# A two-layer graph network on one core: transposed rows written over x, 16 tiles not stored, four groups of moments

## The chip, the cores and the metric

One core of a Trainium2 chip runs the whole kernel. The metric is the device time of one launch in microseconds (us). Before the change it is 4124.46 us, the median of 3 runs (4123.27 to 4125.03).

## The reference, cut to what matters

x has 6250 nodes with 512 features; 100,000 edges (src, dst) are sorted by dst. A graph attention layer with 8 heads of 64 features and then two graph convolutions follow:

```python
h = maximum(layernorm(x), 0)
el = ((h @ W_src + b_src) * attn_l) summed over the 64 features of each head      # [N, 8]
er = ((h @ W_dst + b_dst) * attn_r) summed likewise                               # [N, 8]
v  = h @ W_val + b_val
e  = leaky_relu(el[src] + er[dst]); a = softmax of e over the edges with one dst
x  = x + segment_sum(v[src] * a, dst)
h  = maximum(layernorm(x), 0)
x  = x + relu(gcn(relu(gcn(h, W1, b1)), W2, b2))     # gcn gathers rows by src, too
```

The kernel folds attn into the weights (16 columns instead of 2 x 512), so that el and er come from one narrow product of h, and adds b_val at the end.

## The kernel before, in words

The nodes are cut into 49 tiles of 128 (`TILES`). On-chip memory is nearly full, so areas are reused: `big` (49 x 520 columns a partition) holds first x, then tables of the edge work, then the sums; `rows_wmat` holds 8 slots of 512 columns and the weights; `edge` holds the folding, the search, and later the scores of all edges. Every engine runs its own program in order and waits on semaphores.

**First pass (VectorE, ScalarE, TensorE, SyncE).** x arrives in chunks of 8 tiles, three issued by ScalarE, the rest by SyncE (L1005). VectorE takes the statistics of each tile (L466) and computes mean and deviation for a group of tiles at once (`moments`, L468; groups 0 to 7, 8 to 23, 24 to 48); ScalarE takes the root of a group in `deviations` (L1321). Tile after tile, ScalarE normalizes into one of two slots (L1333), TensorE transposes (`turn`, L1524), and ScalarE copies the transposed tile to one of four slots, `ht_out` (L1341). The copy waits until the score product (L1548) and the store to `ht_tab` of the tile four places before are done. The score product of tile t stands right behind the transpose of tile t + 1. Every four tiles ScalarE copies the 16 score columns (L1348) and TensorE turns them (L1556). The score product needs the folded weights: GpSimd multiplies weights with attn (L1206, L1207) once all six loads have landed, and VectorE reduces (L492, L494).

**Search (VectorE, GpSimd).** Where each node's edges begin is found in seven groups of seven tiles: VectorE counts among 255 row ends (`find_rows`, L510), GpSimd gathers one row of 391 dst for each node (L1216), VectorE counts in it (`count_in_rows`, L523), and every group but the first two waits for the counts of the second before it. The last count is followed by index work on VectorE, TensorE (L1579 to L1607) and SyncE.

**Values (TensorE, ScalarE).** v is computed tile by tile: ScalarE reloads the transposed tile from `ht_tab` into a ring of four slots in `big` (L1317), TensorE multiplies by W_val (`value`, L1566), ScalarE copies and stores to `v_tab` (L1361, L1365). The places are written out by hand: `V1` = 14 values before the picking loop, with the index steps between them (7, then 1, 1, 1, 1, 3), and 35 after it. Of these, 5 and then 6 up to `V_AT[0]`, 8 up to `V_AT[1]`, 10 up to `V_AT[2]`; each such place is followed by a carry step that VectorE's scans need. `EXP_AT` is the value before which ScalarE computes the exponentials (L1385), `W_AT` the value counts before each of the eight turns of the edge weights (L1650).

**Picking loop.** 145 steps for 580 of the 782 edge columns: TensorE gets el[src] by products with one-hot columns (L1621), VectorE picks the block (L684 to L697). Meanwhile GpSimd gathers the other 202 columns (`GCOLS`) from `el_tab` (L1239), paced by the loop.

**Edge stage, then gathers.** VectorE scans over all edges for er, the maxima, the exponentials' sums (L767 to L823). After the store of the sums it zeroes `big` in two parts (L838, L841). GpSimd starts gathering rows of v (L1280) when all values are stored; three stages of 782 gathers follow, each with a dense step between.

Of the kernel before, what the change touches and what calls it, by code (L numbers as in the profile page):

```python
# [68 lines left out]
GROUPED = (0, 8, 24, TILES)  # L69
# [5 lines left out]
Q = 4  # L75
# [47 lines left out]
def build(nc, x, src, dst, W_src, b_src, W_dst, b_dst, W_val, b_val, attn_l, attn_r, W1, b1, W2, b2, out):  # L123
    ctx = ExitStack()
    with ctx:
# [140 lines left out]
        below = part(SEEK * (ROW // 2 + 1)).bitcast(BF16).rearrange("p (s n) -> p s n", s=SEEK)  # L266
# [23 lines left out]
        scanned = part.at  # L290
        ht_ring = part(HT * D).rearrange("p (s n) -> p s n", s=HT)
        ringed = part.at
# [11 lines left out]
        g_from = part(CUT.blocks ** 2 * P // 2).bitcast(BF16).rearrange("p (g n) -> p g n", n=CUT.blocks * P)  # L304

# [6 lines left out]
        def ht_out(slot):  # L312
            return rows[:, (4, 5, 0, 1)[slot], :]
# [4 lines left out]
        def first(t):  # L318
# [15 lines left out]
        pad_set, const_set, ident_set, edges_kept, fold_in, edges_in, dst_in = map(sem, (  # L334
            "pad_set", "const_set", "ident_set", "edges_kept", "fold_in", "edges_in", "dst_in"))
# [11 lines left out]
        wval_in, fold_loads = fold_in, 6  # L347
# [13 lines left out]
        ht_kept, low_before = low_in, [16 * len(range(n, TILES, HT)) for n in range(HT)]  # L361
# [41 lines left out]

        def all_kept(eng, pair, per=16):
            eng.wait_ge(pair[0], per * ((TILES + 1) // 2))
            eng.wait_ge(pair[1], per * (TILES // 2))
# [17 lines left out]

        prep, pe_steps = [0], [0]
# [3 lines left out]
        def _(dve):  # L429
# [38 lines left out]
            def moments(n, at):  # L468
# [9 lines left out]
                dve.scalar_tensor_tensor(ln[:, 1, at], ln[:, 3, at], 0.25, ln[:, 2, at], ALU.mult, ALU.add).then_inc(ln_set, 1)  # L478
                dve.wait_ge(std_set, n + 1)
# [6 lines left out]
            moments(0, slice(0, GROUPED[1]))  # L486
            statistics(range(1, 2))

            for s in range(2):
# [6 lines left out]
            dve.wait_ge(folded, 10)  # L496
            statistics(range(2, 3))
            dve.wait_ge(stat_set, GROUPED[2])
            moments(1, slice(GROUPED[1], GROUPED[2]))

# [51 lines left out]
            moments(2, slice(GROUPED[2], TILES))  # L552
# [17 lines left out]

            dve.wait_ge(h_set, TILES)
# [233 lines left out]
            dve.wait_ge(std_set, 4)  # L805
# [204 lines left out]
        def _(sp):  # L1010
# [4 lines left out]
            sp.dma_start(W_src_sb[:, :, :], W_src.rearrange("(k p) n -> p k n", p=P)).then_inc(fold_in, 16)  # L1015
            sp.dma_start(attn_sb[:, 0, :], on_all(attn_l.rearrange("h f -> (h f)"))).then_inc(fold_in, 16)
            sp.dma_start(bsd_sb[:, 0, :], on_all(b_src)).then_inc(fold_in, 16)
            sp.dma_start(W_dst_sb, W_dst.rearrange("(k p) n -> p k n", p=P)).then_inc(fold_in, 16)
            sp.dma_start(attn_sb[:, 1, :], on_all(attn_r.rearrange("h f -> (h f)"))).then_inc(fold_in, 16)
            sp.dma_start(bsd_sb[:, 1, :], on_all(b_dst)).then_inc(fold_in, 16)  # L1020
# [22 lines left out]
            for t in range(TILES):  # L1043
                sp.wait_ge(hT_set, t + 1)
                sp.dma_start(ht_tab[t, :, :], ht_out(t % HT)).then_inc(ht_kept[t % HT], 16)
                if t in (8, 11):
                    sp.wait_ge(edges_kept, 64)
                    load_firsts((8, 11).index(t))
                if t == 22:
                    sp.dma_start(src_flat[:, 0:J], src_rows.rearrange("g e -> (g e)").rearrange(  # L1050
                        "(p j) -> p j", j=J)).then_inc(edges_in, 16)
                if t == 26:
                    sp.dma_start(dst_i, dst_flat).then_inc(dst_in, 16)
                if t == 30:
                    sp.wait_ge(folded, 10)
                    sp.dma_start(wmat[:, :, 0:D], W_val.rearrange("(k p) n -> p k n", p=P)).then_inc(wval_in, 16)
                if t == 36:
# [8 lines left out]
            sp.wait_ge(h_set, TILES)  # L1066
            sp.wait_ge(dve_prep, marks["ends_of_units"])
# [6 lines left out]
            for n in range(HT):  # L1074
                sp.wait_ge(ht_kept[n], 16 * len(range(n, TILES, HT)))
# [105 lines left out]
        def _(pool):  # L1181
# [37 lines left out]
            pool.wait_ge(h_set, TILES)  # L1219
# [90 lines left out]
        def _(act):  # L1310
# [5 lines left out]
            def load_ht(t, slot):  # L1316
                act.dma_start(ht_ring[:, slot, :], ht_tab[ds(t, 1), :, :].rearrange("a p n -> p (a n)")).then_inc(ht_in[slot], 16)  # L1317

            def deviations(n, at):
                act.wait_ge(ln_set, 9 * n + 7)  # L1320
                act.activation(ln[:, 3, at], ln[:, 1, at], ACT.Sqrt, bias=epsc[:, 0:1]).then_inc(std_set, 1)  # L1321
                act.wait_ge(ln_set, 9 * n + 9)
            deviations(0, slice(GROUPED[0], GROUPED[1]))
# [418 lines left out]
```

## Time and profile before

| | |
|---|---|
| median of 3 runs | 4124.46 us (4123.27 to 4125.03) |
| profiled execution | 4119.5 us, span 4117.6 us, granted clock 0.96 |
| busy, share of the span | TensorE 84%, GpSimd 64%, VectorE 55%, ScalarE 43% |
| chain that ended last | TensorE 33%, GpSimd 24%, issue 21%, DMA 12%, VectorE 6% |
| first pass and index work | 0 to 203.8 us |
| picking loop | 203.8 to 538.5 us |
| edge stage | 538.5 to 713.9 us |
| gathers and dense steps | 713.9 to 4117.6 us |

The profile is of one execution and 5 us below the median. Busy shares are means over stages with different limits; for a change in one stage the waits of that stage count. Only 5% of the span (0 to 203.8) is the first pass and its index work, where most of the edit lies.

### The profile page before, as it was taken

The page shows a single profiled execution, that of the slowest core. Times are in us where ns is not written, and L with a number is a line of the kernel's source. Part 1 is how long each engine was busy: PE and PEld are TensorE (multiplying, and loading weights), DVE is VectorE, ACT ScalarE, POOL GpSimd, SP SyncE. Part 2 cuts the span into 40 slices and gives each one's busy share as a digit, 9 for nine tenths or more (in the row PEclk, how much of TensorE's full clock was granted, in tenths as well). Part 3 has the DMA queues.
Part 4 walks back from the last instruction along what each step waited for, and adds up shares of the span by engine and source line. Part 5 has one row for each costly group of instructions (what it writes and reads, how often), then busy time and mean ns, then how long its engine had stood idle before and what let it go on. Part 6 is the DMA issues. An engine that isn't in the chain of part 4 may idle for free.

```text
span 4117.6 us, 54129 instructions
## 1 busy us (share of the span) xinstructions
PE 3452.2 (84%) x14584; PEld 1660.4 (40%) x14584; DVE 2261.8 (55%) x3808; ACT 1782.4 (43%) x4148; POOL 2652.6 (64%) x2781
## 2 busy tenths in 40 slices
PE   5899986777888888897788888888996788888887
PEld 4499943222233333343333333333442333333333
DVE  6599886677778888884222233333552222333336
ACT  4355512445445555454333344444343333444442
POOL 3676501777777777655777777777006777777775
PEclk9999998999999999999999999999998999999998
DMA  8833335777777777665777777777117777777779
GB/s 287 248 67 62 91 96 190 210 210 211 210 210 211 210 211 211 190 205 189 211 210 210 210 210 210 211 210 210 65 67 221 210 211 210 210 211 210 210 209 353
DMA packets 318135, 802.85 MB, mean 195 GB/s; under 512 B 74201, under 2 KB 97899, under 8 KB 316889
## 3 DMA queue, kind: packets, MB, share of 16 engines
q0 software_dynamic: 201216, 630.92, 53.4%
q1 hardware_dynamic: 87149, 115.33, 8.6%
q10 hardware_dynamic: 29580, 54.49, 3.8%
q8 instruction: 67, 1.10, 0.1%
q14 instruction: 123, 1.01, 0.1%
HBM read 713.14 MB, written 88.19 MB: 195 GB/s over the span
## 4 chain that ended last, share of the span: by engine, by line
PE 33%; POOL 24%; issue 21%; DMA 12%; DVE 6%; SPq 1%; POOLq 1%; DVEq 1%; ACT 1%; ACTq 0%
POOL edge L1280 19%; PE mm L1529 8%; DMA edge<-h_tab,src_group 6%; DMA rows_wmat<-v_tab,src_group 5%; POOL rows_wmat L1280 4%; PE sm L1693 4%; PE mm L1621 4%; PE tr L1621 4%; PE mm L1693 4%; PE sm L1566 3%; DVE edge L866 2%; PE tr L1693 2%; PE tr L1524 1%; DVE big L876 1%; DMA ht_tab<-rows_wmat 1%
## 5 line engine op out<-in xcount | busy, mean ns | idle before, releaser
L1280 POOL DMA_INDIRECT edge<-h_tab,src_group x1564 | 1483.7, 949 | 708.8 <-issue 447.2
L1436 ACT ACTIVATE hots<-iota,drel 128x128 f32<-128x128 f32 x1760 | 538.0, 388 | 1174.6 <-PE tr L1693 593.1
L1280 POOL DMA_INDIRECT rows_wmat<-v_tab,src_group x782 | 739.4, 945 | 289.3 <-issue 218.4
L1693 PE MATMUL mm<-edge,hots 128*128 x880 | 446.1, 654 | 195.5 <-SPq L1098 194.7
L1693 PE MATMUL sm<-edge,hots 128*128 x880 | 454.3, 664 | 155.8 <-SPq L1098 153.1
L891 DVE TENSOR_TENSOR big<-big,mm 128x512 f32 x220 | 151.2, 687 | 674.5 <-PE tr L1693 656.7
L891 DVE TENSOR_TENSOR big<-big,sm 128x512 f32 x220 | 151.2, 687 | 620.8 <-PE misc L1693 606.8
L1693 PE MATMUL tr<-edge,hots 128*128 x880 | 395.6, 592 | 0.0
L1693 PEld LDWEIGHTS mm<-edge,hots 128*128 128x128 f32 x880 | 175.7, 208 | 459.8 <-issue 459.8
L1529 PE MATMUL mm<-rows_wmat 128*128 128x512 f32 x784 | 356.8, 599 | 0.0
L1693 PEld LDWEIGHTS sm<-edge,hots 128*128 128x128 f32 x880 | 180.0, 211 | 422.9 <-issue 422.7
L1673 PE MATMUL mm<-edge,hots 128*128 128x512 f32 x592 | 276.2, 605 | 67.6 <-ACT hots L1422 42.4
L1673 PE MATMUL sm<-edge,hots 128*128 128x512 f32 x584 | 275.4, 602 | 54.4 <-issue 27.9
L866 DVE TENSOR_TENSOR edge<-rows_wmat,tr 128x1024 f32<-128x1024 f32 x224 | 271.9, 1215 | 83.6 <-SPq L1098 83.6
L1422 ACT ACTIVATE hots<-eler_hots,ones 128x256 f32<-128x256 f32 x440 | 223.6, 508 | 206.9 <-PE sm L1673 74.4
L866 DVE TENSOR_TENSOR edge<-rows_wmat,misc 128x1024 f32<-128x1024 f32 x216 | 262.5, 1215 | 80.5 <-SPq L1098 80.1
L1417 ACT ACTIVATE eler_hots<-iota,drel 128x128 f32<-128x128 f32 x880 | 298.2, 386 | 0.0
L1239 POOL DMA_INDIRECT edge<-el_tab,src_flat x202 | 193.3, 957 | 106.2 <-DVE rows_wmat L690 50.9
L1439 ACT ACTIVATE hots<-hots,ones 128x1024 f32<-128x1024 f32 x220 | 252.6, 1148 | 7.1
L1693 PEld LDWEIGHTS tr<-edge,hots 128*128 128x128 f32 x880 | 167.3, 190 | 211.9 <-issue 211.9
L1693 PE MATMUL misc<-edge,hots 128*128 x440 | 206.8, 592 | 0.0
L1693 PE MATMUL hist_ps<-edge,hots 128*128 x440 | 206.8, 592 | 0.0
(252 smaller groups left out, 4465.9 us busy)
## 6 DMA issues: line engine op xcount, KB each, us to landing
h_tab<-rows_wmat SPq DMA_DIRECT2D x98, 256.0 KB, 2.0
edge<-h_tab,src_group POOLq DMA_INDIRECT x1564, 3.7
rows_wmat<-low_tab SPq DMA_DIRECT2D x145, 128.0 KB
ht_tab<-rows_wmat SPq DMA_DIRECT2D x49, 256.0 KB
big<-ht_tab ACTq DMA_DIRECT2D x49, 256.0 KB, 2.8
v_tab<-rows_wmat ACTq DMA_DIRECT2D x49, 256.0 KB, 3.0
x_tab<-big SPq DMA_DIRECT2D x49, 256.0 KB, 2.1
rows_wmat<-v_tab,src_group POOLq DMA_INDIRECT x782, 3.7
```

The source lines that it names most:

```text
L866: dve.tensor_tensor(msgs[:, k % MSGS, :, :].rearrange("p c (h f) -> p c h f", f=F), got, weights.unsqueeze(3).to_broadcast([P, 2, H, F]), ...
L891: dve.tensor_tensor(big[:, ds(o, D)], big[:, ds(o, D)], agg_ps[bank][:, :], ALU.add).then_inc(a["acc_added"], 1)
L1239: pool.indirect_dma_start(el[:, at, :], None, el_tab, bass.IndirectOffsetOnAxis(ap=src_flat[:, at:at + 1], axis=0)).then_inc(el_in[n // AH ...
L1280: pool.indirect_dma_start(ring[:, 2 * u + c, :], None, tab, bass.IndirectOffsetOnAxis(ap=src_group[:, n:n + 1], axis=0)).then_inc(a["rows_ ...
L1417: act.activation(dist[:, n % 2, c, :], iota[:, :], ACT.Abs, bias=drel[:, n * 2 + c:n * 2 + c + 1], scale=-1.0).then_inc(a["dist_set"], 1)
L1422: act.activation(onehot[:, n % HOTS, :, :], dist[:, n % 2, :, :], ACT.Relu, bias=ones[:, 0:1], scale=-1.0).then_inc(a["onehot_set"], 1)
L1436: act.activation(group_hots[:, q % 2, e, :], iota[:, :], ACT.Abs, bias=drel[:, col:col + 1], scale=-1.0).then_inc(a["dist_set"], 1)
L1439: act.activation(group_hots[:, q % 2, :, :], group_hots[:, q % 2, :, :], ACT.Relu, bias=ones[:, 0:1], scale=-1.0).then_inc(a["onehot_set"], 1)
L1529: last = nc.tensor.matmul(bank, rows[:, slot, k * P:(k + 1) * P], rhs(k), start=(k == 0), stop=(k == KC - 1))
L1621: last = pe.matmul(sum_ps[bank][:, q * NA * H:(q + 1) * NA * H], src_hot[:, par, kt, q * P:(q + 1) * P], el_parts[:, part, kt, :, :], star ...
L1673: last = pe.matmul(gat_ps[w % GAT_SUMS][:, :], onehot[:, w % HOTS, n, :], msgs[:, w % MSGS, n, :], start=(n == 0), stop=(n == 1))
L1693: last = pe.matmul(agg_ps[bank][:, :], group_hots[:, q % 2, w % GROUP * 2 + n, :], edge[:, ds(slot[w % OFFS] + n * D, D)], start=(n == 0), ...
```

## The change: what it does

- `ht_out` and its ring of four are gone. ScalarE copies the transposed tile over x, `first(t)` in `big`, without waiting for a store or a product. SyncE stores only tiles 0 to 32 (`STORED`). The score product of tile t now stands behind the transpose of tile t + 12 (`LAGGED`), and the small turns seven steps later.
- Values go in the order of `V_ORDER`: first tiles 33 to 48, read from `big` where they lie, then 0 to 32, reloaded. `V1` becomes 16. The ring of reloads moves from `big` to four slots of `rows_wmat`; two of these are in use in the picking loop, so their first reload is issued at its end.
- Groups of moments: 0 to 7, 8 to 15, 16 to 31, 32 to 48. `moments` is cut in two, `moments` and `scales`, and ScalarE takes the root one step earlier. Folding is done side by side: each side needs three loads. VectorE's order is written anew, with the parts of the search between the statistics. GpSimd waits for the fold before it gathers.
- The places `V_AT`, `EXP_AT`, `W_AT` and SyncE's small loads are shifted. `all_ht_kept` (a wait for all stores) guards `big` before it is reused. Zeroing covers 2048 columns less on VectorE and more on GpSimd.

```diff
-GROUPED = (0, 8, 24, TILES)
+GROUPED = (0, 8, 16, 32, TILES)
-V1 = 14
-V_AT = (V1 + 11, V1 + 19, V1 + 29)
-EXP_AT = (V1 + 25, V1 + 25)
-W_AT = (V1 + 32, V1 + 32, V1 + 33, V1 + 33, V1 + 34, V1 + 34, TILES, TILES)
+STORED = 33
+V1 = TILES - STORED
+LAGGED = 12
+V_AT = (V1 + 11, V1 + 18, V1 + 28)
+EXP_AT = (V1 + 23, V1 + 23)
+W_AT = (V1 + 31, V1 + 31, V1 + 32, V1 + 32, TILES, TILES, TILES, TILES)
+V_ORDER = (*range(STORED, TILES), *range(STORED))
...
-        ht_ring = part(HT * D).rearrange("p (s n) -> p s n", s=HT)
-        ringed = part.at
+        scanned = ringed = part.at
...
-            return rows[:, (4, 5, 0, 1)[slot], :]
+        def reloaded(slot):
+            return rows[:, (6, 7, 2, 3)[slot], :]
...
+            dve.wait_ge(stat_set, GROUPED[2])
+            moments(1, at_group[1])
+            fold_side(0)
+            scales(1, at_group[1])
             turned()
-            for g in range(4):
-                find_rows(g)
-            statistics(range(GROUPED[2] // XL, TILES // XL))
+            find_rows(0)
+            fold_side(1)
+            statistics(range(2, 4))
+            dve.wait_ge(stat_set, GROUPED[3])
+            moments(2, at_group[2])
+            find_rows(1)
+            scales(2, at_group[2])
+            statistics(range(GROUPED[3] // XL, TILES // XL))
...
-            moments(2, slice(GROUPED[2], TILES))
+            moments(3, at_group[3])
+            find_rows(2)
+            scales(3, at_group[3])
+            find_rows(3)
+            dve.wait_ge(folded, 10)
...
-            for t in range(TILES):
+            for t in range(STORED):
                 sp.wait_ge(hT_set, t + 1)
-                sp.dma_start(ht_tab[t, :, :], ht_out(t % HT)).then_inc(ht_kept[t % HT], 16)
+                sp.dma_start(ht_tab[t, :, :], first(t)).then_inc(ht_kept[t % HT], 16)
...
+                if t == 14:
+                    sp.wait_ge(folded, 10)
+                    sp.dma_start(wmat[:, :, 0:D], W_val.rearrange("(k p) n -> p k n", p=P)).then_inc(wval_in, 16)
...
-            pool.wait_ge(fold_in, 16 * fold_loads)
             for s, w in enumerate((W_src_sb, W_dst_sb)):
+                pool.wait_ge(fold_in[s], 16 * fold_loads)
...
             pool.wait_ge(edges_kept, 64)
+            pool.wait_ge(folded, 10)
...
-                    if t >= HT:
-                        act.wait_ge(eler_sum, t - (HT - 1))
-                        act.wait_ge(ht_kept[t % HT], t // HT * 16)
-                    act.activation(ht_out(t % HT), tr[t % 2][:, :], ACT.Copy).then_inc(hT_set, 1)
+                    act.activation(first(t), tr[t % 2][:, :], ACT.Copy).then_inc(hT_set, 1)
...
+            values(0, V1 - 1)
+            all_ht_kept(act)
+            act.wait_ge(eler_turned, -(-TILES // 4))
+            for n in range(2):
+                load_ht(n)
+            values(V1 - 1, V1)
...
-                if 1 <= k <= TILES:
-                    t = k - 1
+                if LAGGED <= k < TILES + LAGGED:
+                    t = k - LAGGED
...
+            def value(c):
+                t = V_ORDER[c]
+                if c < V1:
+                    pe.wait_ge(hT_set, t + 1)
+                    source = first(t)
+                else:
+                    pe.wait_ge(ht_in[t % HT], t // HT * 16 + 32)
+                    source = reloaded(t % HT)
```

## Rows read from the trace of the kernel before

**Rows 1.** Busy us (instructions) by engine in stages; then clock, DMA share, GB/s.
```profile
56.40:138.50 82.10, 75.70 (x564) 53.41 (x562) 63.62 (x223) 58.51 (x96) 46.40 (x49) 0.93 0.79 271
...
203.80:538.50 334.70, 326.87 (x6960) 325.78 (x6960) 298.69 (x862) 192.25 (x288) 204.72 (x216) 0.98 0.31 69
...
713.90:1700.00 986.10, 805.77 (x1759) 298.89 (x1760) 781.66 (x878) 494.31 (x1356) 743.12 (x786) 0.99 0.73 209
```

**Rows 2.** The chain of waits: start us, us, what (whole kernel).
```profile
145.88 25.92 PE sm L1566 x56
...
587.87 30.20 PE sm L1566 x64
619.65 20.81 PE sm L1566 x48
...
688.19 8.87 DVE big L838
699.80 4.67 PE sm L1566 x8
```

**Rows 3.** Who waited for whom, 56.4 to 138.5 (us in total, times, longest).
```profile
ACT rows_wmat L1341 <- DMA ht_tab<-rows_wmat: 11.6, 6, 4.6
```

**Rows 4.** Timeline to 57: start, us, engine, line, out<-in [idle before <-releaser].
```profile
23.99 4.85 DVE L466 BATCH_NORM_STATS2 big<-big  x8 [6.03 <-DMA big<-x]
26.82 1.27 POOL L1206 TENSOR_TENSOR edge<-edge 128x512 f32<-128x512 f32 x1 [23.08 <-DMA edge<-L_gnn_b_dst]
...
31.89 2.46 DVE L492 TENSOR_REDUCE rows_wmat<-edge 128x8 f32<-128x512 f32 x4 [3.05 <-POOL edge L1207]
...
40.69 1.89 PE L1548 MATMUL sm<-rows_wmat 128*16 128x128 f32 x8 [19.85 <-DVE blr L494]
...
53.99 1.12 PE L1524 MATMUL tr<-ident,rows_wmat 128*128 128x128 f32 x4
...
55.04 1.89 PE L1548 MATMUL sm<-rows_wmat 128*16 128x128 f32 x8
...
56.47 0.81 ACT L1333 ACTIVATE rows_wmat<-big,small 128x512 f32<-128x512 f32 x1 [0.53 <-DVE small L482]
```

**Rows 5.** Timeline, 58 to 173: the pass at full clock, the search, index work.
```profile
58.49 0.66 PE L1524 MATMUL tr<-ident,rows_wmat 128*128 128x128 f32 x4
...
59.08 1.05 PE L1548 MATMUL sm<-rows_wmat 128*16 128x128 f32 x8
...
59.30 0.17 DVE L513 CAST er_idx<-small 128x7 int32<-128x7 f32 x1
...
60.06 0.42 PE L1556 MATMUL mm<-ident,rows_wmat 16*128 16x16 f32 x4
...
61.82 0.95 POOL L1216 DMA_INDIRECT edge<-dst_rows,er_idx  x1 [0.30 <-issue]
...
138.50 1.04 DVE L566 TENSOR_TENSOR eler_hots<-mm,blr 128x512 f32<-128x512 f32 x2 [11.36 <-PE mm L1556]
...
172.41 0.21 DVE L613 COPY small<-misc 128x49 f32<-128x49 f32 x1 [11.84 <-PE misc L1580]
```

**Rows 6.** Timeline of the edge stage, 618 to 720.
```profile
618.40 0.41 DVE L713 COPY big<-misc 8x256 f32<-8x256 f32 x1 [3.83 <-PE misc L1657]
...
632.50 6.87 DVE L803 TENSOR_TENSOR edge<-edge 128x3128 f32<-128x3128 f32 x2
...
641.49 1.28 ACT L1385 ACT_TABLE_LOAD   x1 [0.41 <-ACT rows_wmat L1361]
...
660.60 0.38 PE L1657 MATMUL misc<-ident,tail_st 128*8 128x128 f32 x2 [4.58 <-DVE tail_st L812]
...
706.73 3.60 PE L1566 MATMUL sm<-rows_wmat,big 128*128 128x512 f32 x8
...
713.88 0.95 POOL L1280 DMA_INDIRECT rows_wmat<-v_tab,src_group  x1 [51.36 <-DMA v_tab<-rows_wmat]
714.29 5.18 DVE L841 MEMSET big<- 128x6144 f32 x1 [1.91 <-issue]
```

More of the change, by code:

```diff
@@ L402, in all_landed, with all_ht_kept @@
                     eng.wait_ge(pair[b], 16 * n)
+        def all_ht_kept(eng):
+            for n in range(HT):
+                eng.wait_ge(ht_kept[n], low_before[n])
         def all_kept(eng, pair, per=16):
@@ L485, in _, with fold_side @@
             dve.wait_ge(stat_set, GROUPED[1])
-            moments(0, slice(0, GROUPED[1]))
+            moments(0, at_group[0])
+            scales(0, at_group[0])
             statistics(range(1, 2))
-            for s in range(2):
+            def fold_side(s):
                 dve.wait_ge(dve_setup, 2 * s + 2)
@@ L1380, in _ @@
             pipelined(act, PCOLS // Q, 4, 0, far)
+            act.wait_ge(el_picked, PCOLS // Q)
+            for n in range(2, HT):
+                load_ht(n)
             def exponentials(half):
@@ L1530, in product @@
                 last.then_inc(done, 1)
-            for k in range(TILES + 8):
+            for k in range(TILES + LAGGED + 7):
                 if k < TILES:
@@ L1548, in _ @@
                         last = pe.matmul(sm[q % 2][0:2 * H, n * P:(n + 1) * P], wmat[:, kc, D:D + 2 * H],
-                                         ht_out(t % HT)[:, kc * P:(kc + 1) * P], start=(kc == 0), stop=(kc == KC - 1))
+                                         first(t)[:, kc * P:(kc + 1) * P], start=(kc == 0), stop=(kc == KC - 1))
                     last.then_inc(eler_sum, 1)
-                if k >= 8 and k % 4 == 0:
-                    q = k // 4 - 2
-                    pe.wait_ge(elerT_set, q + 1)
-                    for t in range(4 * q, min(4 * q + 4, TILES)):
-                        at = t % (D // (2 * H)) * 2 * H
-                        last = pe.transpose(mm[t // (D // (2 * H))][:, at:at + 2 * H], elerT[:, q % 2, t % 4 * P:(t % 4 + 1) * P],
-                                            ident[0:2 * H, 0:2 * H])
-                    last.then_inc(eler_turned, 1)
@@ L1560, in value @@
-            def value(s):
-                t, par = s.k, s.j % 2
-                pe.wait_ge(ht_in[s.j], (t - s.j) * 4 + 32)
-                if s.past(2):
-                    pe.wait_ge(v_set, t - 1)
+                if k >= LAGGED + 7 and (k - LAGGED - 7) % 4 == 0:
+                    q = (k - LAGGED - 7) // 4
+                    if q * 4 < TILES:
+                        pe.wait_ge(elerT_set, q + 1)
+                        for t in range(4 * q, min(4 * q + 4, TILES)):
+                            at = t % (D // (2 * H)) * 2 * H
+                            last = pe.transpose(mm[t // (D // (2 * H))][:, at:at + 2 * H], elerT[:, q % 2, t % 4 * P:(t % 4 + 1) * P],
+                                                ident[0:2 * H, 0:2 * H])
+                        last.then_inc(eler_turned, 1)
@@ L1565, in value @@
+            pe.wait_ge(elerT_set, -(-TILES // 4))
+            def value(c):
+                t = V_ORDER[c]
[5 more added lines that the diff above has]
+                    source = reloaded(t % HT)
+                if c >= 2:
+                    pe.wait_ge(v_set, c - 1)
                 for k in range(KC):
-                    last = pe.matmul(sm[par][:, :], ht_ring[:, s.j, k * P:(k + 1) * P], wmat[:, k, 0:D],
+                    last = pe.matmul(sm[c % 2][:, :], source[:, k * P:(k + 1) * P], wmat[:, k, 0:D],
@@ L1571, in values @@
             def values(n):
-                for t in range(values_done[0], values_done[0] + n):
-                    value(Step(t, t % HT, TILES, False))
+                for c in range(values_done[0], values_done[0] + n):
+                    value(c)
                 values_done[0] += n
-            pe.wait_ge(wval_in, 16 * (fold_loads + 1))
+            pe.wait_ge(wval_in, 16)
             values(7)
```

104 lines of the change are left out of this document (49 added, 55 removed).

## The prediction

> **What bounds the kernel now.** I read the busy table by stage first [rows 1]. From 713.9 to 1700 GpSimd issues row gathers at 1.25 us each (0.95 busy, 0.30 between), 743 us busy of 986. The two later gather stages are of the same kind, and nothing after 713.9 is edited. So the change can only move the start of that first gather, and what it moves is handed on one to one. The question is what the first 713.9 us wait for.
>
> The chain of waits [rows 2] answers in four pieces. (a) The first pass over the 49 tiles of x ends at 138.5. (b) TensorE then computes "values" (h times W_val, 8 matmuls a tile, 3.45 us at full clock: 20.81/6), 56 matmuls without a break from 145.88, and its index work stands behind them; the picking loop starts at 203.8 [rows 1]. (c) That loop, 203.8 to 538.5, is TensorE at 327 us of 335; it is not edited. (d) From 538.5 VectorE scans and TensorE's values alternate on the chain: the blocks of 64 and 48 matmuls at 587.87 and 619.65 are values, 688.19 is the zeroing of the sums, and 699.80 the value before the last.
>
> In the first pass the tiles pass ScalarE and TensorE; the list of waits shows that ScalarE stood 11.6 us in six waits for the store of an older transposed tile after 56.4 [rows 3]. The timeline shows the start [rows 4]: statistics of chunk 1 at 23.99, the folding product on GpSimd only at 26.82 (after six loads), the first score product at 40.69, tile 8's normalization at 56.47. At full clock a tile costs TensorE 0.59 us for the transpose and 0.98 for the score product (start of one to start of the next, 58.49 and 59.08), and every fourth tile 0.34 to 0.42 more [rows 5].
>
> **The change, part by part.**
>
> *Moments in four groups, fold in two halves.* VectorE now runs: statistics of chunk 1 to 28.8, moments 0.95, fold of one side 3.1 (four reductions 2.46, one 0.68), scales 0.5, one part of the search 3.1 (56.35 to 59.47), fold of the other side 3.1. GpSimd's first product took 5.1 us (26.82 until VectorE took it at 31.89 [rows 4]) and the second somewhat more; the second can still only start at 26.8, so both are ready by 33 and hide. The folds end at 39.8, against 40.6: no gain there. But tiles 8 to 15 get their scale at 33.4 instead of 56.4, and need no score product before them, since that now lags 12 tiles. ScalarE takes 1.43 us a tile (58.5 us busy for 41 tiles [rows 1]), so they are through by 45. Then it is idle again: two chunks of statistics (9.7), moments, a part of the search and the scales put tile 16 at 54.2. The pass is then 8 transposes further than before but has only 4 score products done.
>
> *Rest of the pass.* 33 transposes at 0.59, 45 score products at 0.98 and 13 small turns at 0.34: 19.5 + 44.1 + 4.4 = 68 us from 54.9. I add 2 us for a slow start (a tile at the lower clock costs 1.05 + 1.8 [rows 4], and the clock is low for one or two tiles after a pause) and 1 for the last handshake: end at 126, before 138.5. What makes 82 us become 71: 11.6 us of store waits are gone (the copy goes over x, no ring), and 8 transposes (4.7 us) are done early, against 4 more score products still owed (3.9). The stores that remain (33 of 256 KB) have nothing waiting on them before 126, and SyncE can issue the first 16 from 42 on; at the stage's 271 GB/s they need 32 us. The copy's new target and the product's new source are not in the trace: nearest rows 0.60 and 1.05, and I take no difference.
>
> *Search for rows.* It starts at 39.8 (GpSimd waits for the fold, whose area it overwrites) instead of 61.8, pauses from the second group (ends 62.5) for VectorE's count at 76, and 35 gathers of 1.25 after it are through by 125 at worst, when counts delay it. Not late.
>
> *Values without a reload.* The 7 values before the index product need no DMA: they start at 126.2, behind the pass, and end at 150.4 (7 x 3.45). Before, they started at 145.88 and the product was followed by VectorE at 172.41, which had stood 11.84 us [rows 5]: VectorE was done at 160.6, 22.1 us after the pass. Now that is 148.1, so TensorE is still last, by 2 us. Shift: 171.6 - 150.4 = 21.2 us. Then the order to the picking loop is the old one with two values more (16 instead of 14): +6.9. The loop starts 14.3 us earlier. Its own time stays; the gathered columns and their pacing are the same. The two reloads into slots that the loop occupies are issued at its end, 7 us before TensorE needs them.
>
> *Values between the scans.* The second block shrinks from 8 to 7. VectorE stood 3.83 us at 618.40 for TensorE [rows 6], so one value less gives min(3.45, 3.8) = 3.4 us. Then the exponentials are placed one value sooner after it (5 instead of 6). ScalarE began them at 641.49, 0.41 us behind its copy of a value, while their argument was there at 635.9 (half of the 6.87 from 632.50); a value less gives 3.4 us. TensorE had then 4.58 us to spare at 660.60, of which 1.1 is left: enough.
>
> *End.* Two values stood behind the zeroing of the sums, which ended at 697.1 [rows 2]; the gathers at 713.88 waited 51 us for GpSimd, released by the store of the second. Now only one stands there, so the last store leaves at the end of the product at 699.80 + 4.67 instead of 706.73 + 3.60: 5.9 us. VectorE's last zeroing (6144 columns, 5.18 us) shrinks to 4096 (3.45) and starts earlier too; the first product of gathered rows can't be due before two gathers and a landing, some 5 us behind the first gather, so it is covered, and would cost at most 2 us if not.
>
> Sum: 14.3 + 3.4 + 3.4 + 5.9 = 27.0 us. The profiled execution took 4119.5 us, which becomes 4092.5. The median of the runs is 4124.46, 5 above it, and I forecast against it: 4097.5.
>
> By the Trainium skill's "TensorE: Matmul & The Clock Gate" (section on the HAM clock gate) the low clock is the default and only activity lifts it, which speaks against the new pause of TensorE from 45 to 54. The trace agrees on the size, 3.0 us at low clock for transpose and score product against 1.71 [rows 4, 5]; by the rule alone the cost would be the second rival below.
>
> **Rivals.**
> 1. *Only the first half and the end pay.* If TensorE or ScalarE fills the 3.8 and 4.6 us of slack differently (values stall on their stores, or the exponentials hold ScalarE while TensorE needs its banks), the two 3.4 us are lost: 4104. If VectorE's index chain were not earlier at all, it would be ready at 160.6 and the loop would gain 171.6 - 160.6 - 6.9 = 4.1 instead of 14.3: 4108, or 4114 with both.
> 2. *The clock stays low in the pass (slower).* Place: TensorE from 54.2. A tile there costs 1.3 us more at the low clock, a score product of the tail 0.8. For all 33 tiles and the tail that is 52 us, 25 us net slower: 4150. It decides from 21 tiles on. Against it: after every pause before, two tiles were enough, and the pass had 0.93 of the clock granted [rows 1].
> 3. *Nothing arrives.* If something besides values held the loop or the gathers (the 9 us landing of tables, the sums' store), the gain would be taken up: 4120. The waits named in rows 5 and 6 speak against it.
> 4. *More.* Without slow start, and with the idle time before tile 16 shorter than I count: 4088.
>
> **How the numbers follow.** Forecast as summed, within 6 us: 0.60. Rival 1: 0.20. Rival 4: 0.08. Rival 3: 0.06. Rival 2: 0.04. The rest, 0.02, is a slowdown that I don't see. The cost of the slow start (0 to 6 us) and rival 1 set the range 4086 to 4114, which leaves out under 2 in 10. A measurement of this kernel tells about 0.2%, 8 us, from no change. Rival 3 and part of rival 1's far end lie within it: same 0.08; slower 0.05; faster 0.87.
>
> **What would show it.** In the profile after: the last score turned near 126; no wait of the copy for a store; tile 16's normalization near 54; the first value straight behind the pass; VectorE's wait for the index product near 2 us instead of 11.8; the picking loop at 189 to 190, as long as before; VectorE's wait after the second block near nothing; the exponentials right behind their argument; the first gather near 687, one value after the zeroing. I am wrong if the loop starts after 200, or if the gathers start earlier by 27 us and the rest takes it back.

## The result, and the profile after

The changed kernel takes 4104.6 us by the median of four executions (4099.5 to 4112.6), beside 4124.7 for the kernel before on the same chip: 20.1 us less, ratio 0.995 (0.9937 to 0.9962). A second set of five gave 4099.8 beside 4117.7, ratio 0.9949 (0.9935 to 0.9962). The forecast was 27.0 less, 4097.5: the first median lies 7.1 above it and inside the stated range (4086 to 4114), the second 2.3 above. The profiled execution took 4099.5 (span 4097.7) against 4119.5 (span 4117.6), 19.9 less by the spans.

**Stages.** The first view is the busy table, columns as in [rows 1]: the pass from tile 16 on, the picking loop, the first gather stage.

```profile
56.00:123.90 67.90, 67.49 (x544) 50.14 (x542) 52.31 (x184) 48.66 (x81) 32.07 (x35) 0.99 0.71 241
187.60:527.50 339.90, 327.54 (x6960) 326.02 (x6960) 297.55 (x863) 192.24 (x288) 206.74 (x217) 0.98 0.30 68
688.60:1676.00 987.40, 809.61 (x1768) 300.59 (x1767) 780.62 (x879) 495.95 (x1360) 745.26 (x786) 0.99 0.72 208
```

TensorE is busy 67.5 of 67.9 us in the pass (before: 75.7 of 82.1). The loop starts 16.2 us earlier than before (187.6 for 203.8), yet it and its exit (the stretch from the last full step to VectorE's first instruction behind the loop) need 340 us for the same 327 of TensorE, 5 more than the 335 of before. The first gather starts 25.3 us earlier (688.55 for 713.88), and of these 19.9 arrive at the end.

**The start.** Timeline of after to 60, columns as in [rows 4].

```profile
17.59 1.26 POOL L1226 TENSOR_TENSOR edge<-edge 128x512 f32<-128x512 f32 x1 [13.84 <-DMA edge<-L_gnn_b_src]
...
27.04 4.51 POOL L1227 TENSOR_TENSOR edge<-edge 128x2048 f32<-128x2048 f32 x1
27.98 3.60 DVE L478 TENSOR_TENSOR small<-big 128x8 f32<-128x8 f32 x1
35.61 0.81 ACT L1356 ACTIVATE rows_wmat<-big,small 128x512 f32<-128x512 f32 x1 [1.79 <-DVE small L493]
...
41.02 0.68 DVE L506 TENSOR_REDUCE blr<-edge 128x8 f32<-128x512 f32 x1
...
42.53 1.64 PE L1574 MATMUL sm<-big,rows_wmat 128*16 128x128 f32 x8
...
53.30 1.11 PE L1550 MATMUL tr<-ident,rows_wmat 128*128 128x128 f32 x4 [6.00 <-ACT rows_wmat L1356]
...
55.76 0.81 ACT L1356 ACTIVATE rows_wmat<-big,small 128x512 f32<-128x512 f32 x1 [2.04 <-DVE small L493]
```

Tile 8 is scaled at 35.61 (forecast 33.4), the folds end at 41.7 (39.8), tile 16 is scaled at 55.76 (54.2). The 2 us are one row: an addition of 8 columns on VectorE that takes 3.60 us and ends with GpSimd's product of 2048 columns (27.04 + 4.51). The same line took 0.17 us at 16.41, before GpSimd's first product. The 6.00 us in which TensorE stands are not the wait for tile 16, as I took them to be, but for tile 15, whose normalization stands on ScalarE behind the root of the next group.

**From the pass to the loop.** The same view (timeline) of the later stretch, columns as in [rows 5].

```profile
80.06 0.26 DVE L491 RECIPROCAL small<-small 128x17 f32<-128x17 f32 x1 [9.93 <-ACT small L1343]
...
123.94 1.04 DVE L586 TENSOR_TENSOR eler_hots<-mm,blr 128x512 f32<-128x512 f32 x2 [1.28 <-PE mm L1583]
...
133.31 1.77 POOL L1237 DMA_INDIRECT edge<-dst_rows,er_idx  x1 [0.30 <-issue]
...
147.97 0.32 PE L1612 MATMUL misc<-small,shift 128*128 128x49 f32 x2
...
152.70 0.63 PE L1620 MATMUL misc<-ident,edge 128*128 128x128 f32 x4 [0.44 <-DVE hist L637]
...
187.56 4.63 PE L1654 MATMUL mm<-big,edge 128*128 128x104 bf16 x67 [2.88 <-ACT edge L1401]
```

The pass ends at 123.94 instead of 138.50 [rows 5] and no copy waits for a store. The chain of waits of after (columns as in [rows 2]) runs elsewhere than before:

```profile
111.73 3.88 DVE hots L530 x14
133.31 3.73 DMA edge<-dst_rows,er_idx
139.67 3.88 DVE hots L530 x14
167.32 17.38 PE sm L1599 x40
```

Up to 78 it is still TensorE's pass; from 80.5 to 143.5 it is VectorE's counts and GpSimd's gathers for the search, the last of which ends at 135.1; at the end it is the five values in a row that stand last before the loop.

**The edge stage.** Timeline, columns as in [rows 6].

```profile
519.10 0.88 DVE L705 TENSOR_SCALAR edge<-rows_wmat,low_id 128x512 bf16<-128x512 f16 x3 [10.84 <-remote]
527.56 1.14 DVE L761 TENSOR_SCALAR big<-big,tile 128x256 f32<-128x256 int32 x4
...
603.42 0.41 DVE L734 COPY big<-misc 8x256 f32<-8x256 f32 x1 [0.54 <-PE misc L1690]
617.54 6.87 DVE L824 TENSOR_TENSOR edge<-edge 128x3128 f32<-128x3128 f32 x2
623.07 1.28 ACT L1411 ACT_TABLE_LOAD   x1 [0.39 <-ACT rows_wmat L1375]
642.23 0.38 PE L1690 MATMUL misc<-ident,tail_st 128*8 128x128 f32 x2
679.08 1.97 PE L1683 MATMUL tr<-ident,edge 128*128 128x128 f32 x8 [11.68 <-DVE edge L855]
680.85 4.21 PE L1599 MATMUL sm<-rows_wmat 128*128 128x512 f32 x8
688.55 0.95 POOL L1302 DMA_INDIRECT rows_wmat<-v_tab,src_group  x1 [44.40 <-DMA v_tab<-rows_wmat]
691.91 3.47 DVE L862 MEMSET big<- 128x4096 f32 x1 [1.75 <-issue]
696.92 2.35 DVE L887 TENSOR_TENSOR edge<-rows_wmat,tr 128x1024 f32<-128x1024 f32 x2 [1.53 <-SPq L1118]
```

And three rows of before at the loop's exit, from its timeline:

```profile
528.56 0.88 DVE L684 TENSOR_SCALAR edge<-rows_wmat,low_id 128x512 bf16<-128x512 f16 x3 [3.85 <-remote]
533.23 0.88 DVE L684 TENSOR_SCALAR edge<-rows_wmat,low_id 128x512 bf16<-128x512 f16 x3 [2.67 <-PE tr L1621]
539.25 0.88 DVE L740 TENSOR_SCALAR big<-big,tile 128x256 f32<-128x256 int32 x3
```

Up to its wait "remote" (a wait for which the profile names no releaser) VectorE needs 321.0 us of the loop in before and 320.7 in after; from there to the first instruction behind the loop (539.25, 527.56) it needs 14.5 and 19.3. So the steps cost the same and the exit is dearer. VectorE's one row does not measure this: before waits a second time, 2.67 us for TensorE, and after doesn't.

Behind the exit 11.7 us are left (16.2 less 4.5), the wait at the second carry falls from 3.83 to 0.54, the exponentials are 18.4 earlier [rows 6], and the first gather 25.3.

### The profile page after: what moved, and what is told of

Same layout as the page of the kernel before. It is cut to its first block, busy times and chain, and to the rows that moved or that the text cites. A ratio compares the mean times of both kernels' runs of the same rounds, so it can differ in the third digit from the quotient of the medians.

```text
span 4097.7 us, 54022 instructions
## 1 busy us (share of the span) xinstructions
PE 3458.8 (84%) x14584; PEld 1665.2 (41%) x14584; DVE 2264.1 (55%) x3817; ACT 1782.7 (44%) x4149; POOL 2664.8 (65%) x2781
## 4 chain that ended last, share of the span: by engine, by line
PE 31%; POOL 25%; issue 21%; DMA 13%; DVE 8%; POOLq 1%; ACT 1%; DVEq 1%; ACTq 0%; SPq 0%
POOL edge L1302 19%; PE mm L1555 8%; DMA rows_wmat<-v_tab,src_group 6%; POOL rows_wmat L1302 5%; DMA edge<-h_tab,src_group 5%; PE sm L1726 4%; PE mm L1654 4%; PE tr L1654 4%; PE mm L1726 3%; DVE edge L887 2%; PE tr L1726 1%; PE sm L1599 1%; PE tr L1550 1%; PE hist_ps L1726 1%; PE misc L1726 1%
## 5 line engine op out<-in xcount | busy, mean ns | idle before, releaser
L1726 PE MATMUL mm<-edge,hots 128*128 x880 | 457.9, 669 | 206.0 <-SPq L1118 204.8
```

Of the source, the lines that this page charges most:

```text
L1726: last = pe.matmul(agg_ps[bank][:, :], group_hots[:, q % 2, w % GROUP * 2 + n, :], edge[:, ds(slot[w % OFFS] + n * D, D)], start=(n == 0), ...
```

## The experiments

Lines are those of after. Where an expectation speaks of idle time "ahead of tile 16", it is the 6.00 us above.

**before_again and after_again**, both kernels unchanged.

> The kernel before, unchanged, looked at once more. What differs between the two profiles of before and after in code that the change did not touch: the first three thousand row gathers (median 946 ns before, 949 after), and the stall of all engines at the exit of the picking loop (VectorE stood 3.85 us there before, 10.84 after). Theory A, both belong to one execution: this profile shows another median gather than 946 ns by 2 ns or more, and another stall than 3.9 us by 2 us or more. Theory B, they belong to the kernel (its code and its addresses): 946 ns and 3.9 us come again, within 1 ns and 0.5 us.

> The kernel after, unchanged. Time 4104.5 by its median so far; single executions between 4099 and 4113. Theory A (run to run): the loop exit costs VectorE another time than 10.84 us, by 2 us or more, and the median gather is not 949 ns again. Theory B (the kernel's own): 10.8 us and 949 ns come again, and the first gather starts at 688.5 within 1 us.

4119.6 us (one execution) and 4099.8 (median of five). VectorE stood 4.19 and 10.74 us at the exit. The median gather is 946 ns in both, where the first profile of after had 949. The mean gather of the first and of the later stages is 945 and 949 ns in before_again, as in before, and 946 and 950 in after_again, where the first profile of after had 948 and 952. From the first gather to the last the profiles need:

```
before 3367.9   before_again 3369.0   over_x 3368.1   after 3375.4   after_again 3368.8
```

So the 7 us that the first profile of after lost in the gathers belong to that execution (theory A, in after alone). The stall at the exit belongs to the kernel (theory B): 4.19 for 3.85 and 10.74 for 10.84. Of the two repeats the first gather is at 714.25 and 689.69: 24.6 us earlier.

**over_x**, in the kernel before:

```
-  act.wait_ge(eler_sum, t - (HT - 1)); act.wait_ge(ht_kept[t % HT], t // HT * 16)
-  act.activation(ht_out(t % HT), tr[t % 2][:, :], ACT.Copy)
+  act.activation(first(t), tr[t % 2][:, :], ACT.Copy)      # stores and score products read first(t)
+  # VectorE, SyncE and GpSimd wait for all stores before they write big again
```

> The kernel before with one part of the change: the transposed row is written over its tile of x, scored and stored from there, so the copy waits for no older store and no older score product. All 49 tiles are still stored and read again, groups of moments, fold, lag of one and all places as before. Theory 1 (what the prediction counted): the 11.6 us of waits for stores are pure loss on TensorE's path; the pass then ends at 127 instead of 138.5. Theory 2: the stage is bound by TensorE's work after 56 us and by the DMA of x and of the rows together; the waits only moved the stores, which now queue behind the pass, and the reload (which waits for all of them) ends less than 4 us earlier. The first 56 values start at 145.88 before: by theory 1 at 134, by theory 2 at 142 or later. The whole by theory 1: 10 to 12 us less (ratio 0.9972), if VectorE's index chain, 11.8 us ahead at 172.41, allows it; by theory 2 under 4 us (0.999 to 1.000).

4113.0 us (4110.8 to 4118.6, n = 11) beside 4117.7: ratio 0.9985 (0.9976 to 0.9994). Timeline of over_x:

```profile
127.00 1.04 DVE L566 TENSOR_TENSOR eler_hots<-mm,blr 128x512 f32<-128x512 f32 x2 [5.22 <-PE mm L1557]
...
135.18 5.46 PE L1567 MATMUL sm<-rows_wmat,big 128*128 128x512 f32 x6 [8.21 <-DMA big<-ht_tab]
...
162.96 0.21 DVE L615 COPY small<-misc 128x49 f32<-128x49 f32 x1 [13.22 <-PE misc L1581]
```

Theory 1 holds for the stage and not for the whole: the pass ends at 127.0, 11.5 us earlier, and the values start at 135.2 behind 8.2 us of reload, but the median is only 4.7 less instead of 10 to 12 (ratio 0.9972 lies outside the interval). One of TensorE's waits in before, from its timeline:

```profile
113.38 1.89 PE L1548 MATMUL sm<-rows_wmat 128*16 128x128 f32 x8 [3.59 <-ACT rows_wmat L1341]
```

That the 11.5 meet the 11.6 of ScalarE's waits is partly luck. From its first score product to the pass's end TensorE itself stood three times in before (3.08, 2.77 and 3.59 us, 9.4 in all) and once in over_x (3.3). Behind such a wait tiles run at the low clock (the product above takes 1.89 us instead of 1.05): from 56.4 to the pass's end the granted clock was 0.93 in before and 0.98 in over_x, which I estimate at 5.7 and 1.4 us lost. So 6.1 of the 11.5 are waits and some 4 are clock.

Against before_again 9.9 us are left at the loop (194.31), 8.4 at the first gather (705.84) and 9.4 at the last; this kernel's loop exit is slower too (below).

**old_places**, in after:

```
-V_AT = (V1 + 11, V1 + 18, V1 + 28)
-EXP_AT = (V1 + 23, V1 + 23)
-W_AT = (V1 + 31, V1 + 31, V1 + 32, V1 + 32, TILES, TILES, TILES, TILES)
+V_AT = (V1 + 11, V1 + 19, V1 + 29)
+EXP_AT = (V1 + 25, V1 + 25)
+W_AT = (46, 46, 47, 47, 48, 48, TILES, TILES)
```

> The kernel after with the places of values, exponentials and weight turns as they were before: 8 values in the second block instead of 7, the exponentials 25 values in instead of 23, two values behind the zeroing of the sums instead of one. The prediction's terms: second carry +3.4 us (VectorE waits about 3.9 instead of 0.54 before it), exponentials +3.4 (they start 0.4 behind a copy instead of with their argument), first gather +5.9. Sum 12.7, first gather at 701 and time 4117. Rival: some of it overlaps (ScalarE waits with the exponentials for their argument anyway), and the sum is 6 to 9.

4108.5 us (4104.4 to 4111.8, n = 6), 8.7 over after. Its timeline:

```profile
606.36 0.41 DVE L734 COPY big<-misc 8x256 f32<-8x256 f32 x1 [3.16 <-PE misc L1690]
629.44 1.28 ACT L1411 ACT_TABLE_LOAD   x1 [0.39 <-ACT rows_wmat L1375]
```

With its loop exit at 527.87 (0.3 later than after), the second carry is worth 2.6 us, the exponentials 3.4 more (6.1 together), and the first gather, at 701.38, 6.4 more: 12.5 in all, as forecast (12.7). They add; the rival falls. The last gather is 11.7 later than in after_again. The medians show less (8.7), but they scatter by as much as the difference.

**lag5**, in after:

```
-LAGGED = 12
+LAGGED = 5
```

> The kernel after with the score products 5 tiles behind the transposes instead of 12. Theory 1 (the one I hold since the trace of after): from 56 us to the pass's end TensorE works without a gap (67.6 busy of 68.0), so the pass ends earlier by what TensorE gets done before. With a lag of 12 it stands idle for 6.0 us ahead of tile 16 while 8 score products are owed; with 5 it would fill that time: pass ends at 118 to 120 instead of 123.8. Theory 2 (the change's own ordering is right): the lag keeps tiles 8 to 15 free of the folds, and with 5 TensorE stands before the first score product from 29 to 42 and has ten transposes more to do behind it; the pass ends at 124 or later, up to 130. What the whole gains by theory 1 is bounded by VectorE, which has 0.4 us to spare before the turns of the low bits: 0 to 5 us; by theory 2 it loses 0 to 7.

4103.3 us (4100.0 to 4105.0, n = 5), 3.5 more than after_again (on another chip; the first gather, at 695.72, is 6.0 to 7.2 later than in the two profiles of after). Timeline of lag5:

```profile
85.64 0.27 DVE L491 RECIPROCAL small<-small 128x17 f32<-128x17 f32 x1 [11.58 <-ACT small L1343]
...
150.08 0.50 PE L1612 MATMUL misc<-small,shift 128*128 128x49 f32 x2 [3.65 <-DVE small L615]
...
151.09 6.68 PE L1599 MATMUL sm<-rows_wmat,big 128*128 128x512 f32 x8
```

Neither theory as written. TensorE had its last score turned at 122.1, 1.7 earlier, but ScalarE's last root came 5.6 us later (behind more tiles at TensorE's pace), VectorE's counts with it, and TensorE then waited for the positions: 3.65 us, and one value behind the wait took 6.68 instead of 3.70. The loop began at 193.9, 6.3 later than in after. So what bounds this stage in after is the search on VectorE and GpSimd, as the chain above says, and the lag of 12 pays by letting ScalarE reach that root early.

**last_value**, in after:

```
-W_AT = (V1 + 31, V1 + 31, V1 + 32, V1 + 32, TILES, TILES, TILES, TILES)
+W_AT = (V1 + 31, V1 + 31, V1 + 32, TILES, TILES, TILES, TILES, TILES)
```

> The kernel after with the last value ahead of the fourth weight turn instead of behind it. TensorE stands idle from 667.4 to 679.1 there, for VectorE's copies behind its 8.9 us zeroing; a value takes 4.2. Theory 1: the last value's store, and nothing else, starts the gathers: the first gather starts at 676 to 678 instead of 688.5 (-12), the gathers then run out of ring buffers after 12 of them (15 us, at 691) until VectorE's first message, which comes at 692 to 693 instead of 696.9, since TensorE's last turns follow at once. Net gain 6 to 10 us. Rival: the first gathers are held by VectorE and the weights anyway, the ring fills and what was gained is given back: under 3 us.

4091.1 us (five executions from 4088.1 to 4095.2; a sixth took 6261 at a mean granted clock of 0.73, and its cause is open), ratio 0.9931 (0.9918 to 0.9944), 8.7 less than after. GpSimd's rows:

```profile
673.07 0.95 POOL L1302 DMA_INDIRECT rows_wmat<-v_tab,src_group  x1 [28.85 <-DMA v_tab<-rows_wmat]
...
696.36 0.94 POOL L1302 DMA_INDIRECT rows_wmat<-v_tab,src_group  x1 [8.61 <-DVE edge L887]
```

The gathers start 15.5 us earlier, twelve of them fill the ring, and the thirteenth waits 8.6 us for the first message: the thirteenth is at 696.4, where in after it is at 703.6. The last gather is 10.3 earlier than in after_again. Theory 1, and the first gather 3 to 5 us earlier than it said: the product ended at 669.6, not 671.6, and the gather followed 3.5 us behind, as in after.

**two_after**, in after (all other places keep their numbers):

```
-V1 = TILES - STORED
+UNSTORED = TILES - STORED
+V1 = UNSTORED - 2
...
+  pool.wait_ge(v_sum, UNSTORED)            # ahead of GpSimd's zeroing of big
-  if c >= V1 and V_ORDER[c] + HT < STORED:
+  if c >= UNSTORED and V_ORDER[c] + HT < STORED:
-  if c < V1:
+  if c < UNSTORED:
```

> The kernel after with 14 instead of 16 values ahead of the picking loop; the last two unstored tiles stay in place and their values follow the loop. Theory: VectorE has its first picks ready at 168 to 170 and stands 21.3 us, so the loop is held by TensorE's five values in a row (167.25 to 184.7) alone: it starts 6.9 us earlier, at 180.7. Behind it TensorE has 4.64 us to spare before the first carry and now needs 6.9: 2.3 given back. First gather 4.6 us earlier than 688.5, whole 4 to 5 us less. Rival: VectorE or the far hot vectors of ScalarE (which wait for their table's landing) hold the loop at 185 or later, and the two values are then pure cost behind it: 0 to +2 us.

4093.7 us (4090.0 to 4094.9, n = 5). The loop starts at 180.50 (7.1 earlier, as forecast: nothing but TensorE's values held it), VectorE leaves it at 520.62; but the third carry stands at 642.82 (642.23 in after) and the first gather at 689.38. TensorE then had almost no gap between 521 and 643 (2.5, 1.6 and 2.4 us), so the 7 us were spent at the exponentials and the third carry, where VectorE now stood 3.5 us for TensorE (0.54 in after), and not the 2.3 at the first. The median is 6 us under after's all the same, which the first gather does not explain; the scatter of both is that large.

**padded**, in after, ahead of L1546:

```
+  for _ in range(32):
+      pe.matmul(hist_ps[:, 0:1], ones[0:1, :], lasts[:, 0:1], start=True, stop=True)
```

> The kernel after with 32 one-column matmuls on TensorE at its start, where it idles from 10.6 to 19.8 us: no work is changed, but TensorE's program is longer ahead of the picking loop. It asks what makes all engines stand at the loop's exit, 10.7 us in after and 9.3 in over_x but 3.9 to 4.2 in before. Theory A (where TensorE's instructions lie in memory when it leaves the loop): the stall changes by 2 us or more, and the whole with it. Theory B (something else of the stage): it stays 10.4 to 10.9 us, and the time is that of after.

4098.3 us (4094.8 to 4099.7, n = 5), ratio 0.9946 (0.9934 to 0.9959), that of after. VectorE stood 7.34 us at the exit instead of 10.74 to 10.84, but part of it came back in TensorE's next gaps. From the first match of the loop (TensorE's first product in it) to VectorE's first instruction behind it, in all profiles:

```
before 335.5, 335.0   best 337.5   over_x 337.7   padded 338.6   filled 339.7   old_places 339.9
after 340.0, 340.2    two_after 340.1   moved 340.3   last_value 340.4   lag5 340.5   burst 340.7
```

So instructions added on TensorE ahead of the loop, in time in which it is idle, change the exit by 1.5 us, more than the 0.5 us by which a repeat differs. best, which differs from moved in TensorE's and ScalarE's first pass only, is 2.8 under it. That this comes from where the instructions lie, and that it makes the whole 4.6 us between before and after, is a guess that no run settles. VectorE's own row is a bad measure of it, as two rows of two_after show:

```profile
505.87 0.88 DVE L706 TENSOR_SCALAR edge<-rows_wmat,low_id 128x512 bf16<-128x512 f16 x3 [4.58 <-remote]
...
513.18 0.88 DVE L706 TENSOR_SCALAR edge<-rows_wmat,low_id 128x512 bf16<-128x512 f16 x3 [5.32 <-PE tr L1656]
```

Its wait "remote" is 6 us shorter than in after, and a second wait takes it all back.

**moved**, in two_after:

```
-V_AT = (UNSTORED + 11, UNSTORED + 18, UNSTORED + 28)
-EXP_AT = (UNSTORED + 23, UNSTORED + 23)
-W_AT = (UNSTORED + 31, UNSTORED + 31, UNSTORED + 32, UNSTORED + 32, TILES, TILES, TILES, TILES)
+V_AT = (UNSTORED + 10, UNSTORED + 17, UNSTORED + 26)
+EXP_AT = (UNSTORED + 22, UNSTORED + 22)
+W_AT = (UNSTORED + 29, UNSTORED + 30, UNSTORED + 30, TILES, TILES, TILES, TILES, TILES)
```

> The kernel after with the values placed where TensorE has room: 14 ahead of the picking loop (as in two_after), 12, 7 and 9 ahead of the three carries instead of 11, 7 and 10, the exponentials 5 values behind the second carry as before, and in the turns of the weights one value between the first and the second, three between the third and the fourth (TensorE stands 3.7 and 11.7 us there in after). Theory: two_after lost its 7 us at the exponentials and the third carry, which stood behind too many values, so that TensorE had no gap from 521 to 643; last_value won 15.5 us at the first gather, of which GpSimd stood 8.6 for a free ring buffer, so its last value may be 3 to 6 us later for nothing. Both together: third carry at 636 instead of 642.2, first message 7 us earlier than last_value's 694.3, time 4083 to 4086. Rival: the two do not add, since TensorE becomes the bound between the loop and the third carry (two_after's 4.8 us stay lost): 4089 to 4092.

4084.2 us (4079.2 to 4087.6, n = 4) beside 4120.5, ratio 0.9911 (0.9895 to 0.9926). The parts add: loop at 181.82, third carry at 638.1 (forecast 636), and

```profile
672.66 0.95 POOL L1304 DMA_INDIRECT rows_wmat<-v_tab,src_group  x1 [32.64 <-DMA v_tab<-rows_wmat]
690.28 5.74 DVE L888 TENSOR_TENSOR edge<-rows_wmat,tr 128x1024 f32<-128x1024 f32 x5 [1.53 <-SPq L1119]
692.30 0.94 POOL L1304 DMA_INDIRECT rows_wmat<-v_tab,src_group  x1 [4.94 <-DVE edge L888]
```

the thirteenth gather is at 692.3, 11 us earlier than in after. The last gather is 12.6 earlier than in after_again. The first message came 4.1 earlier than last_value's 694.34, not 7.

**burst** is after with the tiles scored in step k of TensorE's first loop changed; **best** is burst and moved; **filled** is moved with its own steps and one value more ahead of the turns of the low bits (the small turns are moved to match in all three):

```
-after:   k - 12
+burst:   k = 12 to 15: k - 12;   k = 16, ahead of the turn: 4, 5, 6, 7;   from 17: k - 9
+filled:  k = 12 to 14: k - 12;   k = 15, ahead of the turn: 3, 4, 5, 6;   from 16: k - 9
+filled:  values(2)               # for values(1) ahead of the wait for marks["low"]
```

> The kernel after with four of the eight score products that are owed done in one go ahead of the transpose of tile 16, in the 6.0 us in which TensorE stands idle for its scales; behind it the lag is 9 instead of 12. Unlike lag5 this leaves tiles 8 to 15 ahead of the products and ScalarE's root of the last group where it was. Theory: the pass ends 4 us earlier (119.8 to 120.5 instead of 123.8), and the index product follows by what VectorE allows; lag5 ended the pass at 122.1 and lost 3.7 us there, because the last root came 5.6 us later. If the root comes at 80 again, the loop starts 2 to 4 us earlier (184 to 186) and the time is 4096 to 4098. Rival: VectorE was in step with TensorE at the index product and at the low bits (0.4 us to spare), so the loop starts at 187 again: 4100.

> burst and moved together. If their gains add: 6 to 12 us under after's 4099.8 for the one and 2 to 4 for the other, 4080 to 4084 in all; if VectorE holds the index product, as moved alone.

> moved, with the idle time of TensorE in the first pass really filled. In burst the four products stood behind the transpose of tile 15, which itself waits (tile 15's normalization stands on ScalarE behind the root of its group), so they ran at 54.7 instead of from 47.3 on, and the last root came at 83.8 instead of 80.1. Here the products of tiles 3 to 6 stand ahead of the transpose of tile 15, the lag is 9 from tile 16 on, and one value more stands ahead of the turns of the low bits, since VectorE, which waits for GpSimd's gathers of rows (their counts end at 143.5), has those bits at 152.4 whenever the pass ends. Theory: idle time before tile 15 falls from 6.0 to about 2, the pass ends at 120 instead of 124, the last root comes at 80 to 81, and the picking loop starts 3 to 4 us earlier than moved's 181.8: 178, time 4079 to 4082. Rival 1: VectorE's counts are the bound, the loop starts at 181 to 182: as moved, 4084. Rival 2: the low clock behind the filled stretch or a later last root takes it back: 184 and 4086.

burst took 4098.6 us (4097.4 to 4102.8, n = 5), best 4083.6 (4081.5 to 4087.2), filled 4085.4 (4083.7 to 4087.0, n = 4; ratio 0.9904, 0.9888 to 0.9921). In burst TensorE still stood 5.7 us for tile 15 and did the four products behind that tile's transpose, from 54.7 on; the pass ended at 124.2 and not at 120, the last root came at 83.75, VectorE was late for the low bits by 3.4, and the loop began at 190.8: the theory failed, by the wrong tile. best began its loop at 184.15, 2.3 later than moved, and got 2.8 back by its shorter exit. In filled the products ran from 47.7 on; 1.4 and 2.7 us of idle time stayed, the pass ended at 123.0 (moved: 124.9), the last root came at 82.3, and the loop began at 179.1, 2.7 earlier than in moved. VectorE's first message is 4.3 earlier and the last gather 2.1 (4043.8 for 4045.8). The medians of moved, best and filled can't be told apart. Filling TensorE in the pass bought next to nothing in these runs, as one expects where the other chain bounds the stage.

## Why the prediction was right, and where it was off

- *Fold in halves, groups of moments*: right that the folds gain nothing (41.7 for 39.8). Tile 8 came 2.2 us late, tile 16 1.6 late, by VectorE's 3.60 us row, which I had at 0.2. By the Trainium skill's "SBUF — State Buffer" (section "SBUF: two separate sides") VectorE and GpSimd share a port pair that one instruction holds until it ends; a VectorE instruction with two inputs in SBUF takes part beside a GpSimd instruction that reads SBUF. The two rows above agree: GpSimd's started first, and they end 0.03 us apart.
- *Rest of the pass*: forecast 126, measured 123.9. From the first transpose of tile 16 at 56.63 (forecast 54.9) it took 67.3 us, against the 68 of work alone: of the 3 us for the slow start and the handshake nothing was needed. 11.5 us of the gain are the ring's (over_x), 3.1 the groups, the lag and the rest together. The ring's term, 11.6, was read off ScalarE's waits and hit by luck: of the 11.5 only 6.1 are waits of TensorE, and most of the rest is its clock, which the term does not name.
- *Search for rows*: wrong by 10 us. The forecast "through by 125 at worst", which the sum relied on for VectorE's chain, became 135.1, because the counts for which the third group of gathers waits ended near 88 and not at 76. In before it ended at 139.0, only 3.9 later.
- *Values without reload*: right, the first follows the pass at once, and the index product is at 147.97 (150.4 forecast), 23.7 earlier. But one term failed: VectorE's index chain was to be done 22.1 us after the pass, at 148.1. It was done at 151.6, 27.7 after it and 9.0 earlier than before, since the search held it. VectorE came behind the product instead of 2 us ahead of it, and this cost only TensorE's wait of 0.44 us at the low bits, because a value stood in between: luck, as burst (a wait of 3.4) and lag5 (3.65) show. Loop 16.2 earlier for 14.3.
- *"Its own time stays"*: the step that failed and cost the most. The loop's steps took their time, its exit 4.5 us more (335.5 to 340.0). In every kernel with a changed first pass, over_x too, the exit is dearer than in before (337.5 to 340.7), though no line of the loop was edited. The cause is open.
- *Places*: 3.4 + 3.4 + 5.9 forecast, 2.6 + 3.4 + 6.4 by old_places. TensorE's slack at the third carry went from 4.58 to nothing, which cost nothing yet.
- *Gathers one to one*: right by repeat (24.6 at the first gather, 24.8 at the last). The recorded medians show 20.1 and 17.8: executions of after scatter from 4093 to 4113, and the first profile spent 7 us more in gathers that are not edited. What makes an execution of this kind is open.

So the sum is 16.2 - 4.5 + 3.3 + 3.4 + 6.9 = 25.3 for the forecast 27.0. The two errors inside it cancel in part: 1.9 us more at the loop than forecast, 4.5 less behind it. Rival 1 (second half fails) and 3 (nothing arrives) fall by old_places. Rival 2 falls too: from 56 to 124 the granted clock was 0.99. Of rival 4 half came true: no slow start, but the idle time before tile 16 was longer and not shorter. By the first gather the parts are: ring 8.4, places 12.5, and what is left of 24.6, 3.7, unstored tiles, groups and lag together.

## What to carry to other kernels

A wait counted on one engine is not what its removal gives on another: count the waits and the clock of the engine that bounds the stage. When one engine's stage has been shortened, read the chain of waits anew before shortening it again: here the pass went from TensorE to the search on VectorE and GpSimd, and three attempts to fill TensorE (lag5, burst, filled) gave nothing that the medians show, while values moved into TensorE's idle stretches elsewhere gave 15 us by the medians and 12.6 by the last gather (moved). A release that waits for one last store (the gathers on the last value) deserves the earliest idle slot of its producer, and then the ring behind it sets the gain. Moving work out of one wait needs the slack of all later ones in hand: two_after gave 7 us at the loop and none at the gathers until the later places were moved too.

## What the runs showed of the hardware

- The exit of this loop of 145 steps costs a stall in TensorE, ScalarE and VectorE (VectorE waits "remote", TensorE's matmuls come in twos and threes) of 2.7 to 11.2 us by VectorE's row. The loop with its exit takes 335.0 to 340.7 us over 14 profiles, the same again for the same kernel within 0.5 us, and it changes when instructions are added on TensorE ahead of it (340.0 to 338.6). The Trainium skill's "Runtime: NRT & Kernel Launch" (section "Instruction fetch mechanics") says that instructions reach an engine by DMA in blocks of 256 and that a taken branch to one outside the blocks held waits for the fetch. The trace does not bear this out: from 508 to 519 us, in the stall, the DMA table of after has no packet on any queue, and two instruction packets follow later, between 519 and 536. No run here shows what the stall waits for.
- TensorE's clock fell after a wait of 3.65 us: in lag5 the granted clock from 151 to 158 us was 0.56, near the lower of its two levels (1.2 of 2.4 GHz), and a value took 6.68 us instead of 3.70. The wait was thus paid nearly twice.
- TensorE's clock also fell in before behind its waits for the ring of 3.08 and 3.59 us: the score products at 55.04 and 113.38 took 1.89 us instead of 1.05, and the granted clock from 110 to 127 us was 0.80.
- A tiny VectorE instruction beside a long GpSimd one can take as long as what is left of the latter (3.60 us for 8 columns, against 0.17 for the same line alone; and at 17.92 one of 0.95 us that ends 0.02 us after GpSimd's product of 512 columns).
